# A decoder layer on one NeuronCore: score banks shared by both kinds of scores, feed-forward in the transposes' bank, and a new order of the work

## What is computed

```python
x = layernorm(x + attn(x))        # q, kv = x@W_q.T, x@W_kv.T; FFT per head; both divided by their norm per head;
                                  # kv summed over the tokens so far; product; inverse FFT; @W_o.T
x = layernorm(x + xattn(x, ctx))  # 16 heads, causal softmax(x ctx' / 4) ctx
x = layernorm(x + ffn(x))         # x to -0.5, 0, 0.5 by a threshold, times ternary weights plus a variation
```

## Time and profile before

| | us |
|---|---|
| median of 3 runs | 259.92 |
| lowest, highest | 259.2, 260.36 |
| profiled execution | 258.83 |
| its span | 257.0 |
| busy in the span: PE | 197.5 (77%) |
| DVE | 164.8 (64%) |
| POOL | 126.8 (49%) |
| ACT | 100.2 (39%) |
| mean granted TensorE clock | 0.875 of 2.4 GHz |

### The profile page before, as it was taken

The page is one execution under the profiler, slowest core; times in us unless marked ns, Lnnn a source line. Parts: engine busy times, 40 slices in busy tenths (PEclk is TensorE's granted clock), DMA queues, the critical chain, the costliest instruction groups (busy, mean ns, idle before and its releaser), DMA issues.

```text
span 257.0 us, 4854 instructions
## 1 busy us (share of the span) xinstructions
PE 197.5 (77%) x1631; PEld 123.0 (48%) x1631; DVE 164.8 (64%) x398; ACT 100.2 (39%) x227; POOL 126.8 (49%) x272
## 2 busy tenths in 40 slices
PE   7827338997979797979797979797979787583721
PEld 4603124545646455646464646465655455343510
DVE  3473527388775867777767787758787766825141
ACT  1121111445444535455344536253726263323210
POOL 0421675776564645565646565536555553324311
PEclk9995755999997979999979999889999799859575
DMA  6516600002030303130303121213131100000000
GB/s 191 171 26 194 175 14 0 3 24 82 28 97 23 102 3 104 40 106 26 102 20 102 32 93 38 87 34 92 38 87 49 38 20 3 22 0 20 3 20 20
DMA packets 16840, 14.96 MB, mean 58 GB/s; under 512 B 2352, under 2 KB 14768, under 8 KB 16816
## 3 DMA queue, kind: packets, MB, share of 16 engines
q1 hardware_dynamic: 16816, 14.66, 18.6%
HBM read 12.55 MB, written 2.10 MB: 57 GB/s over the span
## 4 chain that ended last, share of the span: by engine, by line
PE 48%; POOL 16%; DVE 14%; issue 9%; ACT 9%; SPq 2%; DMA 2%; POOLq 0%; ACTq 0%; DVEq 0%
PE p_proj L373 9%; PE p_st L381 8%; PE p_out L390 8%; PE p_proj L482 6%; PE p_sum L507 5%; ACT probs L537 4%; DVE unit L697 4%; POOL probs L282 4%; PE p_ap L397 3%; PE p_st L521 2%; PE p_tr L513 2%; POOL nA L268 2%; DMA ident_s<-ident 2%; DVE x_b L611 2%; POOL rnA L275 1%
## 5 line engine op out<-in xcount | busy, mean ns | idle before, releaser
L282 POOL TENSOR_SCALAR_AFFINE_SELECT probs<-probs 128x512 f32<-128x512 f32 x64 | 41.2, 647 | 37.3 <-ACT probs L537 35.3
L537 ACT ACTIVATE probs<-p_st 128x512 f32<-128x512 f32 x64 | 38.0, 598 | 48.8 <-PE p_st L381 48.8
L632 DVE TENSOR_REDUCE x<-p_ap 128x4 f32<-128x512 f32 x64 | 43.7, 687 | 18.1 <-PE p_ap L397 18.1
L381 PE MATMUL p_st<-x1T,keys 32*128 32x128 f32 x512 | 39.0, 292 | 1.4 <-DVE att L650 1.4
L381 PEld LDWEIGHTS p_st<-x1T,keys 32*128 32x128 f32 x512 | 32.7, 194 | 5.4 <-issue 2.5
L251 POOL TENSOR_SCALAR ve<-mv 128x1 f32<-128x1 f32 x48 | 10.5, 219 | 44.4 <-DVE mv L627 44.3
L373 PE MATMUL p_proj<-w_in,xT_s 128*128 128x512 f32 x60 | 31.4, 650 | 0.0
L253 POOL TENSOR_TENSOR rstd<-ve,power 128x1 f32<-128x1 f32 x48 | 27.2, 567 | 4.0
L482 PE MATMUL p_proj<-w_ffn,xqT_s 128*128 128x256 bf16 x96 | 15.0, 299 | 15.4 <-DVE unit L697 12.0
L390 PE MATMUL p_out<-probs,vals 128*32 128x128 f32 x512 | 26.2, 334 | 0.6 <-POOL probs L282 0.6
L579 ACT ACTIVATE outT_s<-p_out 128x512 f32<-128x512 f32 x16 | 9.6, 597 | 39.6 <-PE p_out L390 39.6
(11 more groups left out here) (80 smaller groups left out, 305.0 us busy)
## 6 DMA issues: line engine op xcount, KB each, us to landing
vals<-ctxV SPq DMA_DIRECT2D x16, 256.0 KB, 2.8
xT_s<-xT SPq DMA_DIRECT2D x16, 128.0 KB, 2.5
x_s<-x SPq DMA_DIRECT2D x16, 128.0 KB, 2.8
keys<-ctxK SPq DMA_DIRECT2D x64, 32.0 KB, 2.2
out<-res SPq DMA_DIRECT2D x16, 128.0 KB, 1.7
wq_s<-w_q SPq DMA_DIRECT2D x1, 256.0 KB, 3.0
dft_s<-dft SPq DMA_DIRECT2D x1, 256.0 KB, 3.2
wkv_s<-w_kv SPq DMA_DIRECT2D x1, 256.0 KB, 4.3
```

Of the source, the lines that this page charges most:

```text
L282: nc.gpsimd.affine_select(out=part, in_=part, compare_op=ALU.is_ge, fill=0.0, base=0, pattern=[[0, GH], [1, TOK]], channel_multiplier=-1). ...
L381: mm = nc.tensor.matmul(p_st[s % 2][:, g * TOK:(g + 1) * TOK], keys[t.b % 4][slot, GH * g + s, :], x1T[slot, g, :], start=True, stop=True)
L537: nc.scalar.activation(probs[:, c, :, :].rearrange("p g q -> p (g q)"), p_st[c % 2][:], ACT.Exp, scale=HD ** -0.5).then_inc(exps[c], 1)
L632: nc.vector.tensor_reduce(x1[(t.b + 1) % 4][:, GH * c:GH * (c + 1), HD], p_ap[c % 2][:].rearrange("p (h k) -> p h k", h=GH), AX.X, ALU.max ...
```

## The change

Seven things change; the function of the program stays.

- Banks: p_st and p_ap (two each) become p_b[0..3]. Chunk c has p_b[c] for its approximate scores of one batch and its exact scores of the batch before, in turn. The transposed outT_s goes back into p_out, and the feed-forward product into half of p_tr.
- The inverse norm's refinement: nA = rsA squared on ScalarE, hA = -0.5 nA ssq and rnA = (hA + 1.5) rsA on VectorE, in place of four operations on GpSimd.
- Offsets: TensorE's step t now has batches t+2 (projection), t+1 (sum over tokens), t (y, w_out, bf16 transposes), t-1 (approximate scores), t-2 (exact scores, weighing), t-3 (transposes of outT_s) and t-4 (feed-forward). The steps run from -2 to 19.
- Order within a step, on all five engines.
- Scores 2 and 3 come before 0 and 1, and one semaphore tells of a pair.
- SyncE: the keys and values of batch t+1 are asked for behind the store of batch t-4.
- The start: GpSimd blanks all keys tiles and converts the constants; the weights' fold is done bank by bank, the first projection stands ahead of w_out's fold, each constant has its own semaphore, and w_out is copied by ScalarE.

```diff
-def steps(step):
-    for b in range(-3, BATCH + 1):
+def steps(step, ahead, behind):
+    for b in range(-ahead, BATCH + behind):
         step(Step(b))
...
-        p_st = [bank(f"p_st{i}", [128, CW]) for i in range(2)]
-        p_ap = [bank(f"p_ap{i}", [128, CW]) for i in range(2)]
+        p_b = [bank(f"p_b{c}", [128, CW]) for c in range(CHUNKS)]
...
-        pv = p_st[1][:].rearrange("p (s g w) -> p s g w", s=GH, g=GROUPS)
+        pv = p_out[:].rearrange("p s (g w) -> p s g w", g=GROUPS)
+        p_ffn = p_tr[:, 0:2, :].rearrange("p a b -> p (a b)")
...
+            def step(t):
+                if t.has(-4):
+                    sp.wait_ge(out_ready, t.done(-3))
+                    sp.dma_start(out[t.batch(-4)], res[t.ring(-4, 2)][:]).then_inc(stored[t.ring(-4, 2)], 16)
+                if t.has(4) and t.batch(4) >= 4:
                     sp.wait_ge(proj, t.done(1))
+                    load_xT(t.batch(4))
                     sp.wait_ge(added[0], t.done(1))
+                    load_x(t.batch(4))
+                if t.has(1) and t.batch(1) >= 4:
+                    sp.wait_ge(pv_done[1], t.done(-2))
+                    load_kv(t.batch(1))
...
+            pool.wait_ge(in_barred, 16)
+            for buf in range(4):
                 nc.gpsimd.tensor_copy(keys[buf][:], barred_s[:].unsqueeze(1).to_broadcast([128, HEADS, TOK])
                                       ).then_inc(keys_blank[buf], 1)
...
-            def refine_norms(t):
-
-                pool.wait_ge(rsA_done, t.done(4))
-                nc.gpsimd.tensor_tensor(nA[:], rsA[:], rsA[:], ALU.mult).then_inc(nA1, 1)
-                pool.wait_ge(nA1, t.done(4))
-                nc.gpsimd.tensor_tensor(nA[:], nA[:], ssq[:], ALU.mult).then_inc(nA2, 1)
...
-            def score(t, pair):
+            def score(buf, first):
 
                 for g in range(GROUPS):
-                    for s in pair:
+                    for s in (first, first + 1):
                         slot = slice(SLOT * s, SLOT * (s + 1))
+                        last = nc.tensor.matmul(p_b[s][:, g * TOK:(g + 1) * TOK], keys[buf][slot, GH * g + s, :],
+                                                x1T[slot, g, :], start=True, stop=True)
+                last.then_inc(scored[first // 2], 1)
...
+                if t.has(-4):
+                    if t.batch(-4) == 0:
+                        pe.wait_ge(ffn_seq, 10)
+                    pe.wait_ge(xqT_copied, t.done(-3))
+                    for g in range(2):
+                        for i in range(3):
+                            last = nc.tensor.matmul(p_ffn, xqT_s[:, g, :], w_ffn[i][:, g, :],
+                                                    start=(g == 0 and i == 0), stop=(g == 1 and i == 2))
+                    last.then_inc(ffn, 1)
...
+                if t.has(4):
+                    act.wait_ge(rsA_done, t.done(5))
+                    nc.scalar.activation(nA[:], rsA[:], ACT.Square).then_inc(rsA_squared, 1)
...
+                if t.has(1):
+                    dve.wait_ge(rsA_squared, t.done(2))
+                    nc.vector.scalar_tensor_tensor(out=hA[:], in0=nA[:], scalar=-0.5, in1=ssq[:], op0=ALU.mult,
+                                                   op1=ALU.mult).then_inc(half_step, 1)
...
+                if t.has(1):
+                    dve.wait_ge(half_step, t.done(2))
+                    nc.vector.scalar_tensor_tensor(out=rnA[:], in0=hA[:], scalar=1.5, in1=rsA[:], op0=ALU.add,
+                                                   op1=ALU.mult).then_inc(rnA_done, 1)
```

More of the change, by code:

```diff
@@ L98, in decoder_layer @@
         sq = sb("sq", [128, 2 * DIM])
-        ssq, lnA, rsA, nA, rnA = (sb(n, [128, 2 * HEADS]) for n in ("ssq", "lnA", "rsA", "nA", "rnA"))
+        ssq, lnA, rsA, nA, hA, rnA = (sb(n, [128, 2 * HEADS]) for n in ("ssq", "lnA", "rsA", "nA", "hA", "rnA"))
         unit = sb("unit", [128, 2, HEADS, 2 * BINS])
@@ L367, in _, with fold_out @@
-            last.then_inc(folded, 1)
+                last.then_inc(folded, 1)
+            def fold_out():
+                pe.wait_ge(in_out, 32)
+                for g in range(2):
+                    for o in range(2):
+                        last = nc.tensor.matmul(p_tr[:, 2 * g:2 * g + 2, :].rearrange("p a b -> p (a b)"),
+                                                idftT_s[:, o, g * 128:(g + 1) * 128], woT_s[:, o, :],
+                                                start=(o == 0), stop=(o == 1))
+                last.then_inc(folded, 1)
@@ new lines, in step @@
+                if t.has(-2):
+                    pe.wait_ge(maxed[0], t.done(-1))
+                    pe.wait_ge(x1T_b_copied, t.done(0))
+                    for g in range(GROUPS):
+                        last = nc.tensor.transpose(p_tr[:, g, :], x1[t.ring(-2, 4)][:, GH * g:GH * (g + 1), :]
+                                                   .rearrange("p h s -> p (h s)"), ident_s[:])
+                    last.then_inc(x1T_done, 1)
+                if t.has(-1):
+                    pe.wait_ge(kv_in[t.ring(-1, 4)], t.filled(-1, GH + 1, 4))
+                    pe.wait_ge(x1T_b_copied, t.done(0))
+                    approximate(t.ring(-1, 4), 1)
@@ new lines, in step @@
+                if t.has(0):
+                    if t.batch(0) == 0:
+                        pe.wait_ge(w_out_ready, 1)
+                    pe.wait_ge(yT_copied, t.done(1))
+                    for g in range(2):
+                        last = nc.tensor.matmul(p_sum[:, 0, :], yT_s[:, g, :], w_out[:, g, :],
+                                                start=(g == 0), stop=(g == 1))
+                    last.then_inc(outA, 1)
+                if t.has(-3):
+                    pe.wait_ge(outT_copied, t.done(-2))
+                    for g in range(GROUPS):
+                        last = nc.tensor.transpose(p_out[:, g, :], outT_s[:, g, :], ident_s[:])
+                    last.then_inc(out_done, 1)
@@ L424, in step @@
+                if t.has(-1):
+                    pe.wait_ge(exps[0], t.done(-1))
+                    approximate(t.ring(-1, 4), 0)
+                if t.has(0):
+                    if t.batch(0) == 0:
+                        pe.wait_ge(consts_b, 5)
+                    pe.wait_ge(x1_b_done, t.done(1))
+                    pe.wait_ge(added[2], t.done(-3))
                     for g in range(GROUPS):
@@ L473, in step @@
-                if t.has(-1):
-                    if t.has(3):
-                        pe.wait_ge(normed, t.done(4))
-                    pe.wait_ge(xqT_copied, t.done(0))
-                    pe.wait_ge(ffn_seq, 10)
-                    for g in range(2):
-                        for i in range(3):
-                            last = nc.tensor.matmul(p_proj[:, 0:DIM], xqT_s[:, g, :], w_ffn[i][:, g, :],
-                                                    start=(g == 0 and i == 0), stop=(g == 1 and i == 2))
-                    last.then_inc(ffn, 1)
@@ L526, in _ @@
+            steps(step, 2, 4)
         @block.scalar
@@ L598, in _ @@
-            steps(step)
+                if t.has(-2):
+                    act.wait_ge(stored[t.ring(-2, 2)], t.filled(-2, 1))
+                    act.wait_ge(shift_done, t.done(-1))
+                    nc.scalar.activation(res[t.ring(-2, 2)][:], r3[:], ACT.Identity, bias=shift3[:],
+                                         scale=rstd[2][:]).then_inc(out_ready, 1)
+                if t.has(1):
+                    act.wait_ge(scored[1], t.done(2))
+                    exponentials(2)
+                    exponentials(3)
+                    act.wait_ge(scored[0], t.done(2))
+                    exponentials(0)
@@ L600, in _ @@
+                if t.has(1):
+                    act.wait_ge(pv_done[1], t.done(2))
+                    nc.scalar.activation(outT_s[:], p_out[:], ACT.Copy).then_inc(outT_copied, 1)
+                if t.has(5):
+                    act.wait_ge(ssq_done, t.done(6))
+                    nc.scalar.activation(lnA[:], ssq[:], ACT.Ln).then_inc(lnA_done, 1)
+            steps(step, 5, 2)
         @block.vector
@@ L736, in dft_tables @@
+            steps(step, 1, 5)
 def dft_tables():
```

622 lines of the change are left out of this document (259 added, 363 removed).

## The result

The changed kernel takes 209.24 us (median of 4 runs, 207.62 to 211.18) against 259.95 us (259.20 to 260.36): a ratio of 0.803, with a 95% interval of 0.798 to 0.809. The forecast was 222.0 us with a range of 208 to 242. The direction came out, and the time lies at the low end of the range, on the case called "better than forecast" (209 us). The profiled execution took 209.64 us with a span of 207.9 us. Ratios leave out a run that is over 1.5% above the fastest of its kernel, while the medians given are those of all runs, so b2 has no ratio (of its four runs one, 251.63 us, would be left), and the profiles of b2 and e2 are of such longer runs.

The account below looks back on a forecast made before the run. TensorE's loop was taken as the bound, VectorE and loads close behind: 10.2 us a period. Filling 50, periods 24 and 102, last three 27, clock 3, tail 13.2 make 219.2; with 1.83 and 1.09, 222 us, range 208 to 242.

Parts of the forecast that it names:

- better than forecast: Rival: PE streams at 9.4 us a period without any stall and clock falls vanish, 209 us; chance 0.08.
- filling: Stage up to the first outT_s copy: put at 50 us, 46 if waits are hidden, 55 if batch 0 is delayed.
- two filling periods: The two periods after the first outT_s copy, still filling: 12 us each, 24 us together.
- ten periods: The full periods in the middle: 10.2 us each, 102 us together, by bounds 9.7 to 10.8 us a period.
- PE's loop: TensorE's own work in a period: 9.8 us, the middle between a count of 9.3 and the busy time 10.38.
- last three: The last three periods: 27 us, a batch's chain taking about 6 us at full clock and 9 at half.
- clock: Falls of TensorE's clock to 1.2 GHz in full periods: two at 1.5 us each, 3 us; none or six possible.
- The stall before the xq transposes: PE waits there for ACT's copy of x1T, 3.95 us of chain against 3.66 of work: 0.3 to 0.4 us a period.
- The loads' loop: From one approximation 1 through result, store, keys and vals to the next: 9.8 us, within half a microsecond of PE's.
- the slower rival: The loads' one-step lead makes their loop the period; equality needs about 13.4 us; 265 us if it happened, chance 0.05.
- The centre of the argument: The 5.15 us detour from PE over ScalarE, GpSimd and unit to the feed-forward explains the 12 us period.
- Contention: Rival: VectorE and GpSimd block each other, four VectorE operations lengthen by 0.3 us each; period 11.3, 235 us; chance 0.22.

Follow-up runs that it names:

- b2: The kernel before with the feed-forward product in p_tr and its waits for unit and r3 removed, order unchanged: 257.31 us, no ratio.
- e2: The changed kernel with each of the four keys transfers split in two, eight in all, order kept: 250.61 us, ratio 0.959 to before.
- e1: The changed kernel with keys and values of batch t+1 asked for ahead of the store of batch t-4: 200.64 us, ratio 0.770 to before.
- e5: The changed kernel with GpSimd's three pieces of feed-forward weights one step earlier, in the gap behind y_done: 199.81 us, ratio 0.766 to before.
- e7: e1 with the banks divided two and two between approximate and exact scores, as in the kernel before: 228.34 us, ratio 0.875 to before.
- b4: The kernel before with the feed-forward in p_tr and the refinement on ScalarE and VectorE, old order and offsets: 248.50 us, ratio 0.953.

## Where the prediction was right, and where it was not

The span was put at 219.2 us and is 207.9. The time, 209.24 us, lies 13 us below the forecast and 1.2 us above the lower end of the range, in a case that had a chance of 0.08. That it lies inside is owed in part to the width of the range, since the argument for the old period was wrong and a filling stage 4.3 us longer than forecast made up for part of what the other terms had too much. Term by term:

| term | put at | measured | what was off |
|---|---|---|---|
| filling | 50 | 54.3 | the weights' pieces on GpSimd |
| two filling periods | 24 | 21.5 | the second is 9.56 |
| ten periods | 102 | 96.0 | PE's loop, 92.3 alone; the loads gave back 3.7 |
| last three | 27 | 23.2 | no half clock |
| clock | 3 | 0 | no fall in the steady part |
| tail | 13.2 | 12.9 | |

**PE's loop.** Put at 9.8 us plus a stall of 0.3 to 0.4; it is 9.23 (e1, every period). This is the term that was mis-sized. The lower of my two counts, 9.3, was right: it took rows of long groups and scaled them by columns. The upper bound, the busy time of 10.38 us, was no bound, since it held more than the work (two groups of scores 1.16 us each, 1.72 as one); in the new order the same matmuls are busy 9.1 us. I had the scores as two at 1.10. The middle of a good number and a bad one cost 0.5 us a period.

**The stall before the xq transposes** did not come. In the steady part of the changed kernel the copy x1T was done 0.1 to 1.1 us before them, and in e1 0.14 us before them in every period, so it is close behind the bound there. What stands there instead is a wait that I had not counted: approximation 2 waits for the exponential that frees its bank. In e1's chain:

```profile
113.55 0.61 ACT probs L494
...
114.21 0.40 PE p_b L368
```

PE fills it with the second pair of scores and stands only 0.14 us in each period. It is the shared bank's own price.

**The loads' loop**, put at 9.8 us, was 9.94 in the stretch quoted, and its links agree within 0.5 us each: 2.53 us for the keys' issues in both, and 3.25 us of landing where I had 2.8. It was called the slower rival, which needed 13.4 us; in truth it became the bound because PE's loop was shorter than I thought. The sentence "if approximation 1 waits for DMA, the loads' loop is the bound" held, and e1 confirmed it. The changed kernel landed at "better than forecast" with a different inner working: PE could go at 9.23, the loads kept it at 9.6.

**The centre of the argument**, that the 5.15 us detour over GpSimd and unit made the old period and that the feed-forward's bank removes it, was wrong (b2: 0.03 us a period). Unit had been done for 0.64 us when the feed-forward began. The longer of the two chains was the one over xq, the scores, an exponential and the copy xqT_s, and it ended 0.10 us before it.

**Contention** did not come on VectorE. xq takes 0.426 us in every period, the short operation hA 0.128 (0.17 in batches 1 to 3), with one exception in batch 0 (duration ns min/median/max, first and last start):

```profile
L588 DVE SCALAR_TENSOR_TENSOR xq<-x,above x16: 424/426/427, 67.2 to 199.9; 128x256 bf16<-128x256 f32 x16
```
```profile
L609 DVE SCALAR_TENSOR_TENSOR hA<-nA,ssq x16: 126/128/1299, 13.8 to 166.0; 128x32 f32<-128x32 f32 x16
```

The mechanism exists, but in the new order the masks lie beside operations of VectorE that read PSUM or have one input. One pair does meet, r2 with its two inputs and, 0.02 us behind it, an inverse root on GpSimd, and there GpSimd pays:

```profile
107.80 0.42 DVE L626 TENSOR_TENSOR r<-att,x 128x256 f32<-128x256 f32 x1
107.82 0.82 POOL L316 TENSOR_TENSOR rstd<-ve,power 128x1 f32<-128x1 f32 x1
```

The same operation takes 0.57 us in the first batches, where r2 is not beside it, and 0.82 in twelve of its sixteen executions. It is the same in e1, where PE's only idle time in a period is 0.14 us behind an exponential, so it costs no time there.

**Filling.** Unit of batch 0 was put at 13.9 us and came at 15.37, hA taking 1.30 us for 0.13. The first copy was put at 50, "55 if the wider pipeline delays batch 0"; it was 54.3, and e5's 47.9 shows that the pieces of the weights are worth 6.4 us up to there and 9.4 in the whole. I had seen them there and put no price on them.

**The clock.** Two falls were assumed in the steady part, none came. The runs order themselves as one would think in part only: no fall in the middle of e1, two in that of e7, where PE stands 1.14 us in one place, and one in seven of ten loops of e2, where it stands up to 3.7 us. But b4, whose PE is busy 10.3 of 11.67 us, has none in its middle either. What decides between b4 and e7 stays open.

## What to carry to other kernels

When a chain of waits ends in one wait for several things, look up when each of them was done before pricing the removal of one: here the chain named unit, 0.64 us early, the copy xqT_s came 0.54 us later, and the 5.15 us of the chain were worth 0.03. A piece of the chain in which nothing is waited for is a sign of it. In a pipeline where each engine's order is fixed, a loop through the DMA queue stays hidden as long as it is shorter than the compute loop, and each gain on the compute side brings it nearer; ask for loads before the queue waits for a result. Work done once at the start belongs where its engine has a gap: moving three pieces of it was worth 9.4 us here.

## What the runs showed of the hardware

**A VectorE operation with two SBUF inputs and a GpSimd operation beside it: in these rows the later one pays.** At the start of the changed kernel hA, 128x32, begins while GpSimd blanks keys tiles:

```profile
11.34 3.73 POOL L236 COPY keys<-barred_s 128x2048 f32<-128x2048 f32 x2
...
13.81 1.30 DVE L609 SCALAR_TENSOR_TENSOR hA<-nA,ssq 128x32 f32<-128x32 f32 x1 [0.82 <-ACT nA L506]
```

The two copies end at 15.07 us and hA, started at 13.81, at 15.11: 1.30 us for 0.13. And the order of the two decides who pays. In the kernel before the mask is first and xq second; xq takes 0.73 us:

```profile
148.95 0.68 POOL L282 TENSOR_SCALAR_AFFINE_SELECT probs<-probs 128x512 f32<-128x512 f32 x1 [0.35 <-ACT probs L537]
...
149.17 0.73 DVE L686 SCALAR_TENSOR_TENSOR xq<-x,above 128x256 bf16<-128x256 f32 x1
```

In b4 xq starts 0.04 us ahead of the mask, and the mask takes 0.88 us, where most take 0.64:

```profile
118.15 0.43 DVE L671 SCALAR_TENSOR_TENSOR xq<-x,above 128x256 bf16<-128x256 f32 x1
...
118.19 0.88 POOL L271 TENSOR_SCALAR_AFFINE_SELECT probs<-probs 128x512 f32<-128x512 f32 x1 [0.61 <-ACT probs L520]
```

The Trainium skill's page "SBUF — State Buffer", section "Who interferes with whom", states that the later of two such instructions is blocked in full. The row of hA agrees to 0.04 us; xq and the mask do not: they were lengthened by 0.3 and 0.24 us, less than what was left of the other (0.46 and 0.39 us). So the price is not the fixed 0.3 us that I took: it was up to 1.2 us here, and nothing for xq where no mask ran ahead of it (0.43 us). No run isolates this; it is read from rows, and GpSimd's ends in them are rough.

**In e2 a long wait and half clock come together, and half clock lengthens the loop.** The eight longest waits for vals in e2, 2.34 to 3.74 us, each had a stretch at 1.2 GHz beginning within 1.5 us of their end; the three of 1.28 us or less had none. PE's groups are links of the loop that the next load hangs on: after the wait of 3.48 us, at 1.2 GHz, it took 14.72 us, 2.3 more than the one after it at full clock. It doesn't build up: the wait at the end of that long loop was 1.28 us, and the loop behind it ran at full clock. The length of a wait alone doesn't tell when the clock falls: b4 stands 0.96 us in every period and its clock stays full in the middle, the kernel before stands 1.00 us and has five falls.
